# Causal attention with the value products of a key tile in two halves of two heads, placed between and behind the score pairs of the next tile

## The reference, cut to what matters

```python
h = layernorm(x, ln_g, ln_b)
q = (h @ q_w).reshape(Bsz, L, H, dh).transpose(0, 2, 1, 3)      # L = 2048, H = 16, dh = 16
k = (h @ k_w).reshape(Bsz, L, KV, dh).transpose(0, 2, 1, 3)     # KV = 4
...
sc = jnp.einsum('bhqd,bhkd->bhqk', q, k) / jnp.sqrt(jnp.float32(dh))
mask = jnp.where(jnp.tril(jnp.ones((L, L), bool)), 0.0, -1000000000.0)
p = jax.nn.softmax((sc + mask).astype(jnp.float32), -1).astype(q.dtype)
o = jnp.einsum('bhqk,bhkd->bhqd', p, v).transpose(0, 2, 1, 3).reshape(Bsz, L, D)
return o @ o_w + res
```

## Time and profile before

| | us |
|---|---|
| median of 3 runs | 4044.51 |
| lowest and highest | 4023.53, 4046.77 |
| the profiled execution | 4019.58 |
| its span in the trace | 4017.7 |
| causal attention in it, first maximum to last value product | 1172 to 2331 |
| banded attention, windows | 3257 to 3742 |

### The profile page before, as it was taken

One profiled execution on the slowest core, in us unless ns is written; L12 is line 12 of the kernel. 1 busy time (PEld: TensorE's weight loads), 2 busy tenths in 40 slices (PEclk: granted clock), 3 DMA queues, 4 the chain that ended last, 5 costly groups with the idle time before them and its releaser, 6 DMA issues. The chain is left out here.

```text
span 4017.7 us, 46219 instructions
## 1 busy us (share of the span) xinstructions
PE 3371.3 (84%) x16242; PEld 1650.9 (41%) x16242; DVE 2484.0 (62%) x5354; ACT 1680.3 (42%) x2670; POOL 1168.8 (29%) x1015
## 2 busy tenths in 40 slices
PE   6899989897668988999988979994997478878799
PEld 2344334342323323333323235552555255555466
DVE  2999999999727768767768613335662244556212
ACT  4556556554213555554555622211121344434332
POOL 2767776667432000221000000000222333311110
PEclk9999999999968999999999989996998688888899
DMA  2222222212141122022121010003122256453100
GB/s 76 74 66 71 70 67 69 67 65 73 48 71 39 25 30 36 26 49 46 21 30 24 10 50 11 11 6 101 62 91 95 80 135 133 119 118 68 35 21 21
DMA packets 187783, 232.16 MB, mean 58 GB/s; under 512 B 56763, under 2 KB 134031, under 8 KB 184195
## 3 DMA queue, kind: packets, MB, share of 16 engines
q1 hardware_dynamic: 184482, 220.84, 21.7%
q0 software_dynamic: 3072, 8.39, 0.7%
HBM read 183.26 MB, written 45.89 MB: 57 GB/s over the span
## 5 line engine op out<-in xcount | busy, mean ns | idle before, releaser
L1287 ACT ACTIVATE g_pT<-PS 128x1024 f32<-128x1024 f32 (+3 forms) x640 | 552.4, 894 | 466.9 <-PE PS L1593 276.7
L379 POOL TENSOR_TENSOR WB<-m_dtx,WB 128x1024 f32<-128x1024 f32 x256 | 600.9, 2351 | 294.3 <-DVE WB L523 262.9
L1433 DVE TENSOR_REDUCE g_mxp<-PS 128x1 f32<-128x512 f32 x768 | 491.8, 686 | 91.4 <-PE PS L1574 87.4
L411 ACT ACTIVATE PS<-m_dt,m_A 128x512 f32<-128x512 f32 x512 | 353.2, 691 | 433.0 <-DVE WB L514 432.4
L1574 PE MATMUL PS<-g_KT,WB 96*128 96x512 bf16 (+3 forms) x1280 | 423.3, 363 | 120.0 <-DVE g_mxp L1433 57.2
L608 PE MATMUL PS<-WB,ident 128*128 128x512 f32 x1024 | 503.0, 614 | 0.0
L514 DVE TENSOR_TENSOR_SCAN WB<-PS,m_state,WB 128x512 f32<-128x512 f32 x384 | 472.2, 1275 | 14.9 <-ACT PS L411 14.7
L1593 PE MATMUL PS<-WB,g_KT 99*128 99x512 bf16 (+3 forms) x1280 | 359.1, 353 | 1.2 <-ACT g_pT L1287 0.6
L1574 PEld LDWEIGHTS PS<-g_KT,WB 96*128 96x128 bf16 x1280 | 110.4, 98 | 503.8 <-DVE g_mxp L1433 260.4
L523 DVE TENSOR_TENSOR WB<-WB,PS 128x1024 f32<-128x1024 f32 x256 | 308.8, 1206 | 5.8 <-PE PS L594 2.4
L1426 DVE CUSTOM_DVE_ANT_0 PS<-PS,g_mq 128x384 f32<-128x384 f32 (+3 forms) x512 | 246.5, 507 | 98.6 <-PE PS L1574 92.0
(11 more groups left out here) (311 smaller groups left out, 5227.8 us busy)
## 6 DMA issues: line engine op xcount, KB each, us to landing
WB<-b_rows SPq DMA_DIRECT2D x256, 256.0 KB, 3.1
WB<-in_L_ffn_w SPq DMA_DIRECT2D x18, 1024.0 KB, 7.5
WB<-g_dq SPq DMA_DIRECT2D x96, 128.0 KB, 4.1
g_rden<-g_dn SPq DMA_DIRECT2D x128, 64.0 KB, 2.0
w_dv<-WA SPq DMA_DIRECT2D x16, 512.0 KB, 4.5
w_V<-w_dv SPq DMA_DIRECT2D x16, 512.0 KB, 10.7
w_rden<-w_dn SPq DMA_DIRECT2D x128, 64.0 KB, 2.1
g_dq<-g_parts SPq DMA_DIRECT2D x16, 384.0 KB, 2.5
```

Of the source, the lines that this page charges most:

```text
L379: pool.tensor_tensor(hh[:, g % RING, :, :], dtx[:, MB * h:MB * h + MB, :], Bs[:, g % BRING, :].unsqueeze(1) .broadcast_to([P, MB, CH]), AL ...
L411: act.activation(PS[:, 2 + b, :], dt[:, c % 2, m, :], ACT.Exp, scale=Aneg[:, n, m:m + 1]).then_inc(dA_ready, 1)
L1287: act.activation(pT[:, n % 2, 2 * pair:2 * pair + 2, 0:width], PS[:, 2 * pair:2 * pair + 2, at:at + width], ACT.Exp, scale=DH ** -0.5).the ...
L1433: dve.tensor_reduce(mxp[:, q % 6, i % QB, hh:hh + per, at], scores[:, :, 0:width], AX.X, ALU.max)\
```

## The change

In the causal attention the value products of a window are two steps, `pv` (n, 0) of heads 0 and 1 and `pv` (n, 1) of heads 2 and 3. The first stands at n + 1.2, which is behind the first pair of turned scores of window n + 1; the second pair moves from n + 0.25 to n + 0.5; the second half stands at n + 1.7, behind that pair. In the closing window of a group the second half stands at n + 1.25, next to the first. The banded attention has its steps at the old places, with the two halves at the same time. The semaphore `pv` counts halves, each half waits for its own pair's exponential, and each exponential for its own half of two windows before.

```diff
         for n, (q, _) in enumerate(self.windows):
-            acts += [(n, "turn", n, 0), (n + 0.25, "turn", n, 1), (n + 1.45, "pv", n)]
+            if causal:
+                closes = n + 1 == self.first[q + 1]
+                acts += [(n, "turn", n, 0), (n + 0.5, "turn", n, 1), (n + 1.2, "pv", n, 0),
+                         (n + (1.25 if closes else 1.7), "pv", n, 1)]
+            else:
+                acts += [(n, "turn", n, 0), (n + 0.25, "turn", n, 1), (n + 1.45, "pv", n, 0),
+                         (n + 1.45, "pv", n, 1)]
...
                             if causal or c == NJ - 1:
-                                sp.wait_ge(pv, first[2 * w + 2])
+                                sp.wait_ge(pv, 2 * first[2 * w + 2])
                             else:
-                                sp.wait_ge(pv, first[2 * w + 3] + 1)
+                                sp.wait_ge(pv, 2 * first[2 * w + 3] + 2)
...
                         act.wait_ge(st, 2 * n + pair + 1)
-                        if pair == 0 and n >= 2:
-                            act.wait_ge(pv, n - 1)
+                        if n >= 2:
+                            act.wait_ge(pv, 2 * (n - 2) + pair + 1)
...
                     elif what == "pv":
-                        n, = x
+                        n, pair = x
                         q = wins[n][0]
-                        if n + 1 == first[q + 1]:
-                            act.wait_ge(pv, n + 1)
+                        if pair and n + 1 == first[q + 1]:
+                            act.wait_ge(pv, 2 * n + 2)
...
                     elif what == "pv":
-                        n, = x
+                        n, pair = x
                         q, (j, at, width, _, _) = wins[n]
                         s, J, g = block_of(q)
                         opens, closes = n == first[q], n + 1 == first[q + 1]
-                        pe.wait_ge(ex, 2 * n + 2)
+                        pe.wait_ge(ex, 2 * n + pair + 1)
                         if opens and q:
                             pe.wait_ge(o_out, q)
-                        for hh in range(4):
+                        for hh in (2 * pair, 2 * pair + 1):
                             mm = pe.matmul(PS[32 * hh:32 * hh + 32, 6, at:at + width],
```

## The result

The changed kernel took 4179.09 us (median of 4 runs, 4174.97 to 4197.01) against 4035.47 us for the kernel before (4 runs): a ratio of 1.0365, 95% interval 1.0317 to 1.0413. Timed again in a later set it stood at 1.0378 (1.0342 to 1.0414). The forecast was 4214 us, in a range of 4130 to 4300. In the profiled execution the span went from 4017.7 to 4173.1 us, by 155.4, where the sum had said 170.

The account below looks back on a forecast made before the run. PE was taken to bound the kernel, DVE second. 280 for halves, 6 for closing windows, less 120 of waits, plus 4 for band attention made +170 us: 4190 profiled, 4214 against the median, range 4130 to 4300.

Parts of the forecast that it names:

- A half costs a whole: Causal value products: two heads cost PE as much as four, 1.09 us at 512 columns; 280 us added over 292 windows.
- the 0.09 ahead: PE's gap ahead of each value group, 0.09 us, counted in its price beside 0.15 us behind.
- rival B: Split causal windows: a half's passes don't pair, three rounds each, 210 us more PE time, 4400 us; chance 0.07.
- The gaps are paid again: Each split causal window pays 0.24 us of gaps around its value products again, 70 us of the 280.
- Rival D's second form: Causal value products: the gaps are not doubled, leaving +100 us; rival D's chance 0.05.
- The 6 and 4 us: PE time taken as added: 6 us in the 28 closing windows, 4 us in the banded attention.
- The 11 and 26 us of the upper bounds: Most that three rounds for two could add: 11 us in closing windows, 26 us in the banded attention.
- What PE gets back: Causal stage: PE's waits for DVE before maxima shrink, returning 120 us, bounds 75 and 165.
- the two thirds behind the 95: Causal stage: beyond 25 us hidden in narrow windows, two thirds of the other 140 us of standing, 95, come back.
- Rival C: Causal stage: DVE's waits stay, little beyond 25 us comes back, +260 us, 4305 us; chance 0.07.
- rival D's first form: Causal stage: waits go entirely and the clock stays full, +115 us, 4138 from the fastest run; rival D's chance 0.05.

Follow-up runs that it names:

- the one-head steps: The changed kernel with its value products in four steps of one head each: 4630.05 us, ratio 1.1489 to the kernel before.
- the two-head groups: The kernel before with the causal value products of heads 2 and 3 of each group left out, order untouched: 4038.4 us, ratio 1.0045.
- the halves that meet in a row: The changed kernel with each window's second half moved directly ahead of the next window's first half: 4060.95 us, ratio 1.0067 to the kernel before.
- the column halves: The changed kernel's order and places, but each half takes all four heads over half the window's columns: 3993.18 us, ratio 0.9920 to the kernel before.
- whole groups between the pairs: The kernel before with four heads in one step but the changed kernel's order, value group at n + 1.2: 4033.54 us, ratio 1.0031.

## Why the prediction was right, point by point

**A half costs a whole.** Right to 0.02 us: 1.08 against the 1.09 that the sum used, and with the 0.09 ahead 0.87, 0.64 and 0.44 for the narrower ones (0.88, 0.66, 0.45). That a round gets no shorter with fewer heads in it was argued from the full-array pass, and the one-head steps, the two-head groups and the halves that meet in a row show it from three sides: PE pays for a round, whether one, two or four column groups are in it. Two heads' passes pair just as four heads' do, so rival B is out.

**The gaps are paid again.** Right. Around the halves and around the column halves stand the same 0.09 to 0.10 us ahead and 0.13 to 0.15 behind; behind a lone head it is 0.12. Rival D's second form, that the gaps need not double, is out by these rows. A rival that the prediction doesn't name is that the gaps come from the change between bf16 and float32, and not from the 32 columns. The trace of the kernel before settles it:

```profile
1610.90 0.60 PE L1593 MATMUL PS<-WB,g_KT 99*128 99x512 bf16 x2
1611.42 0.24 PE L1623 MATMUL PS<-identb,g_mparts 128*48 128x128 bf16 x1
1611.59 0.39 PE L1574 MATMUL PS<-g_KT,WB 96*128 96x512 bf16 x1
...
1613.35 0.60 PE L1593 MATMUL PS<-WB,g_KT 99*128 99x512 bf16 x2
1613.79 1.88 PE L1552 MATMUL PS<-g_hT,WA 128*128 128x512 f32 x4
1615.50 0.38 PE L1574 MATMUL PS<-g_KT,WB 96*128 96x512 bf16 x1
```

The float32 projection over the full array starts 0.44 us after two bf16 products, two steps of 0.22, and four passes of 0.43 later the next bf16 product starts: no gap on either side. The maxima's rows (L1623), bf16 but only 48 columns wide, have 0.08 to 0.10 us more ahead of them and 0.11 behind. The Trainium skill's rule (TensorEngine Tiling (Array Packing), Key Properties), that a change of tiling mode drains the engine, agrees with these rows; the drain itself is not in the trace, only the time that each switch takes.

**Closing windows and the banded attention.** The 6 and 4 us were too much: a second half right behind the first adds nothing (ratio 1.0001 with all of them so), in either stage. The 11 and 26 us of the upper bounds don't exist. The 8 us that the Trainium skill's figure for an increment would give (TensorE: Matmul & The Clock Gate, The cost: per-tile semaphore tail), an estimate for the case that nothing hides them, would be a ratio of 1.0020, just beyond the interval's end of 1.0017; they don't show.

**What PE gets back.** 121 to 128 us against 120 taken, with bounds 75 and 165. The mechanism was right: PE's waits for DVE fell from 93 to 18 us and DVE waits in its place. How it is shared out was off: about 40 us instead of 25 are hidden in the narrow windows, which leaves 80 to 90 for the rest where 95 were taken. The two errors are of opposite sign, and the two thirds behind the 95 were a choice between bounds; that the total came out so near is in part luck. Rival C, waits that stay, would have left PE standing for some 135 us, and rival D's first form, waits that go entirely, for none; it was 37 to 44.

**The sum.** 280 - 128 = 152 in the stretch, 155 in the span. Against it 170 was said: 10 us less for seams that cost nothing, 8 less between the price of the halves and what came back (280 - 120 against 152), and 3 more from the drift of the other stages. The forecast of 4214 lies 35 us over the measured 4179: 9 of them are the base, whose median with a fourth run is 4035 and not 4044.5, and 26 the change, 170 against the 144 between the two medians.

**What stays open.** Why the column halves get back more than their gaps while whole groups between the pairs gain nothing. The traces say where: PE's waits for DVE are 32 us with column halves and 72 with whole groups, and its waits for exponentials 1.5 and 19. Shorter pieces of PE work between the maxima are the reason that was argued, but no experiment varied the length of the pieces with the order held in every other way. The few microseconds by which places in the plan differ are not explained either.

## What to carry to other kernels

In this kernel the small products that share the array side by side are priced by the round and not by the piece. Before moving a part of such a group elsewhere, count how many rounds there will be; if a group has to be cut, cut it along the moving columns, where the rounds get shorter, and not across its members, where they get emptier. What a finer interleaving can return is at most the time that the bounding engine stands still now, and that can be counted before the change: here 165 us to win against 280 to pay.

## What the runs showed of the hardware

- A float32 group of 32-column products took 0.98, 0.99 and 1.00 us to the next start at 512 columns with one, two and four heads in it, and two halves with a wait and an increment between them ran in that same 1.00 us.
- Halves of different windows with different operands also ran side by side (eight records in 0.99 us), a 512-column half beside one of 384 in the 0.99 us of the wider, and sixteen records of column halves, four after four, in 1.00 us. The seam between steps was free each time; where it was looked at, with the halves side by side, the second step's first passes started before the first step's second ones.
- Each time PE went from full-array products to such a group and back it cost 0.21 to 0.24 us, whatever the group's width or number of heads. A bf16 product of 48 columns paid about as much (0.08 to 0.10 and 0.11 us), and a float32 product over the full array between bf16 ones nothing.
